# A two-layer model on one core: the picked experts' tiles fetched, scattered and summed another way, and r read from PSUM

## The reference

```python
# first layer, attention part (RWKV form), 16 heads of 16 channels
h  = rms_norm(x)                      # x is the layer norm of the input
xx = shift_by_one_token(h) - h
r, k, v = (h + xx*mu_r) @ Wr, (h + xx*mu_k) @ Wk, (h + xx*mu_v) @ Wv
decay = exp(-exp(w0 + tanh((h + xx*mu_w) @ wA) @ wB))
for t in tokens:                      # for each head a 16 x 16 state S
    kv = k[t][:, None] * v[t][None, :]
    o[t] = r[t] @ (S + u * kv)
    S = decay[t][:, None] * S + kv
x = x + (group_norm(o) * silu(g)) @ Wo
x = x + gelu(rms_norm(x) @ ffn_w1) @ ffn_w2
# first layer, expert part: 2 shared experts, and the 4 best of 16 for each token
gate = top4(softmax(xt @ router_w.T)) # xt is the layer norm of x
x = x + shared(xt) + sum_e gate[e] * (gelu(xt @ up[e].T) @ down[e].T)
# second layer: a selective scan (512 channels x 16 states), then 2 groups of 32 experts, 2 picked
```

## Time and profile before

| | us |
|---|---|
| median of 3 runs | 5431.09 |
| the profiled execution, own time | 5400.89 |
| its span | 5399.1 |
| PE, DVE, ACT, POOL busy | 4088.6, 3766.1, 2723.4, 3324.5 |
| mean granted clock of PE | 0.876 of full |

### The profile page before, as it was taken

The page is one execution under the profiler, slowest core; times in us unless marked ns, Lnnn a source line. Parts: engine busy times, 40 slices in busy tenths (PEclk is TensorE's granted clock), DMA queues, the critical chain, the costliest instruction groups (busy, mean ns, idle before and its releaser), DMA issues. The chain is left out here.

```text
span 5399.1 us, 63470 instructions
## 1 busy us (share of the span) xinstructions
PE 4088.6 (76%) x18842; PEld 2739.3 (51%) x18842; DVE 3766.1 (70%) x6401; ACT 2723.4 (50%) x5744; POOL 3324.5 (62%) x2226
## 2 busy tenths in 40 slices
PE   5777777877688767778251698889888889759994
PEld 1344445554455534555241465555555555548883
DVE  6888886769777777631000698888888889845677
ACT  1333334543344434446131677777777777525552
POOL 3455554446666566651425888888888888845552
PEclk7877788887798878889676899999999999879997
DMA  3222234333455444542555311221122111187788
GB/s 140 86 97 96 97 116 136 122 127 119 126 161 142 127 140 128 159 129 73 117 127 101 99 54 65 80 85 68 63 79 81 69 66 70 58 252 236 229 282 281
DMA packets 425042, 658.92 MB, mean 122 GB/s; under 512 B 46688, under 2 KB 292832, under 8 KB 414688
## 3 DMA queue, kind: packets, MB, share of 16 engines
q1 hardware_dynamic: 347904, 509.95, 29.5%
q0 software_dynamic: 76800, 144.90, 10.2%
HBM read 450.83 MB, written 213.04 MB: 123 GB/s over the span
## 5 line engine op out<-in xcount | busy, mean ns | idle before, releaser
L1699 POOL TENSOR_TENSOR c_dbx<-c_dtx,c_Brep 128x1024 f32<-128x1024 f32 x512 | 1201.6, 2362 | 182.1 <-DVE c_hs L1717 99.5
L1127 POOL TENSOR_TENSOR a_kv<-a_rk,a_kv 128x512 f32<-128x512 f32 x512 | 731.8, 1447 | 864.4 <-DMA a_kv<-v_rows 852.7
L1717 DVE TENSOR_TENSOR_SCAN c_hs<-psum,c_carry,c_dbx 128x512 f32<-128x512 f32 x768 | 937.4, 1266 | 119.4 <-ACT psum L1706 70.4
L1706 ACT ACTIVATE psum<-c_dt,c_cols 128x512 f32<-128x512 f32 x1024 | 697.2, 688 | 363.2 <-DVE c_hs L1717 358.7
L1136 DVE TENSOR_TENSOR_SCAN a_S<-a_decay,a_carry,a_kv 128x513 f32<-128x513 f32 x512 | 795.5, 1554 | 60.8 <-POOL a_kv L1127 55.5
L1733 PE MATMUL psum<-ident,c_hs 128*128 128x128 f32 x4096 | 609.0, 282 | 110.3 <-DVE c_hs L1717 106.6
L1733 PEld LDWEIGHTS psum<-ident,c_hs 128*128 128x128 f32 x4096 | 486.0, 144 | 393.3 <-DVE c_hs L1717 215.3
L1142 DVE TENSOR_TENSOR a_prod<-a_rk,a_S 128x512 f32<-128x512 f32 x512 | 454.8, 888 | 140.3 <-PE psum L1158 140.3
L1048 POOL DMA_INDIRECT a_xc<-picked_results,a_from_row x192 | 343.1, 1787 | 227.3 <-DMA a_xc<-x 130.4
L2128 POOL DMA_INDIRECT results<-d_ys,d_to_row x320 | 310.9, 972 | 236.1 <-DVE d_to_row L2228 178.6
L892 POOL DMA_INDIRECT picked_rows<-a_row,a_to_row x256 | 342.5, 1338 | 176.5 <-DVE a_xb L705 80.1
(11 more groups left out here) (321 smaller groups left out, 8593.9 us busy)
## 6 DMA issues: line engine op xcount, KB each, us to landing
a_kv<-v_rows SPq DMA_DIRECT2D x512, 256.0 KB
c_Brep<-b_rows SPq DMA_DIRECT2D x64, 1024.0 KB, 4.7
a_t_rows<-picked_rows SPq DMA_DIRECT2D x316, 136.0 KB, 2.3
d_xs<-sorted_rows SPq DMA_DIRECT2D x320, 128.5 KB
picked_results<-a_t_y SPq DMA_DIRECT2D x316, 128.0 KB
d_w<-results SPq DMA_DIRECT2D x64, 512.0 KB, 11.4
d_w<-in_d_experts SPq DMA_DIRECT2D x32, 768.0 KB, 9.4
x<-a_xb SPq DMA_DIRECT2D x20, 512.0 KB, 3.5
```

The lines of the kernel that those rows point to most:

```text
L1127: m_kv[g] = pool.mark(nc.gpsimd.tensor_tensor(kv[:, g % NV, 1:C + 1], rk[slot][:, 1, hb, :], kv[:, g % NV, 1:C + 1], ALU.mult))
L1699: m_dbx[g] = m_dbx[g + 1] = pool.mark(nc.gpsimd.tensor_tensor(dbx[:, r:r + 2, :], dtx[slot][:, e, :].unsqueeze(1).broadcast_to([P, 2, C]), ...
L1706: m_da[g] = act.mark(nc.scalar.activation(psum[:, DA + g % ND, :], dt[slot][:, e, :], ACT.Exp, scale=A[:, e, n:n + 1]))
L1717: m_scan[q] = dve.mark(nc.vector.tensor_tensor_scan(hs[:, q % NR, :], psum[:, DA + q % ND, :], dbx[:, q % NX, :], first, ALU.mult, ALU.add))
```

## The change

Two things are changed in the first layer.

1. Picked experts. The segments are 2, 3, 4, 4 and 3 chunks. A routed row now carries, beside its 16 gates, 16 slot numbers (token x 4 + rank of the pick), so that it is 288 values wide. ACT issues the fetch of each tile. The step's instructions have another order. POOL copies the slot column of a tile to `to_slot` and scatters the tile's results with an indirect DMA to their slots; there are 4 buffers `t_y` and not 2. `combine` is then 4 plain DMAs of POOL for a chunk, DRAM to DRAM, which add the results of pick k to x; each waits for the one before it. The correction of row numbers in `plan`, the gathers, `xc` and the quota are gone.
2. The scan. The ring `G` has 3 banks (5 to 7). Banks 3 and 4 hold r of the current chunk: ACT copies it there (`queries`), and the product behind the scan reads r from the bank. The copy into `carry` is done by ACT.

Besides, the load of `xa` is a generator of its own (`ask_xa`), `SORT_RATE` is 1.0 and not 0.8, and the list of streams is longer.

```diff
+        def ask_xa(c):
+            while now[0] < (c - 2) * steps + steps // 2 or c >= 3 and not is_done(("x1 free", c - 3)):
+                yield
+            load_xa(c)
+            m_done["xa asked", c] = True
...
-        OB, FD, G = 0, Banks(psum, 2, 1), Banks(psum, 3, 5)
+        OB, FD, RB, G = 0, Banks(psum, 2, 1), 3, Banks(psum, 5, 3)
...
+        def queries(c):
+            for hb in range(KB):
+                while not is_done(("r", c)) or c >= 1 and not is_done(("used r", c - 1, hb)):
+                    yield
+                yield from rest(1)
+                act.after(m_done["r", c], m_done.get(("used r", c - 1, hb)))
+                m_done["r bank", c, hb] = act.mark(nc.scalar.copy(psum[:, RB + hb, :], rk[c % 2][:, 0, hb, :]))
...
-                    sp.after(m_T.get(q - NTX), m_ty.get(q - NTX))
-                    nc.sync.dma_start(t_rows[:, q % NTX, :], row_of[bass.ds(at_row.pop(j), 1), :, :].rearrange("a p d -> p (a d)")).then_inc(s_tx[q % NTX], 16)
+                    act.after(m_T.get(q - NTX), m_ty.get(q - NTX), m_slot.get(q - NTX))
+                    nc.scalar.dma_start(t_rows[:, q % NTX, :], row_of[bass.ds(at_row.pop(j), 1), :, :].rearrange("a p d -> p (a d)")).then_inc(s_tx[q % NTX], 16)
...
-                    sp.after(m_ty[q])
-                    nc.sync.dma_start(result_of[j], t_y[:, q % NTY, :]).then_inc(s_ty[q % NTY], 16)
+                    pool.after_alone(m_ty[q], m_slot[q])
+                    nc.gpsimd.indirect_dma_start(out=picked_results[slot], in_=t_y[:, q % NTY, :], in_offset=None,
+                                                 out_offset=bass.IndirectOffsetOnAxis(ap=to_slot[:, q % NTI:q % NTI + 1], axis=0),
+                                                 bounds_check=Z.results - 1).then_inc(s_ty[q % NTY], 16)
...
+                        if q - 3 >= NTI:
+                            pool.engine.wait_ge(s_ty[(q - 3 - NTI) % NTY], 16 * ((q - 3 - NTI) // NTY + 1))
+                        pool.engine.wait_ge(s_tx[(q - 3) % NTX], 16 * ((q - 3) // NTX + 1))
+                        m_slot[q - 3] = pool.mark(nc.gpsimd.tensor_copy(to_slot[:, (q - 3) % NTI:(q - 3) % NTI + 1], t_rows[:, (q - 3) % NTX, E:][:, bass.ds(at_slot.pop(j), 1)]))
...
+            pool.engine.wait_ge(s_store[c % 2], 16 * (c // 2 + 1))
+            for i in range(NTY):
+                pool.engine.wait_ge(s_ty[i], 16 * len(range(i, m_done["tiles", s], NTY)))
+            at = (c - opens[s]) * C * TOP
+            results_of = picked_results[s % 2][at:at + C * TOP, :].rearrange("(p t k) d -> p t k d", t=TL, k=TOP)
             for k in range(TOP):
...
+                if k:
+                    yield from rest(3)
+                    pool.engine.wait_ge(s_sum[c % 4], 16 * (c // 4 * TOP + k))
+                nc.gpsimd.dma_start(chunk_of(chunks_out, c), results_of[:, :, k, :], accum_op=ALU.add).then_inc(s_sum[c % 4], 16)
+                yield
...
-                    dve.after(m_scan[q], m_sum.get((q - NP) // 4 * 4 + 3))
-                    m_prod[q] = dve.mark(nc.vector.tensor_tensor(prod[:, q % NP, :], rk[cq % 2][:, 0, sq_ // DK, :], S[:, q % NS, 0:C], ALU.mult))
+                    dve.after(m_scan[q], m_sum.get((q - NP) // 4 * 4 + 3), m_done["r bank", cq, sq_ // DK])
+                    m_prod[q] = dve.mark(nc.vector.tensor_tensor(prod[:, q % NP, :], psum[:, RB + sq_ // DK, :], S[:, q % NS, 0:C], ALU.mult))
...
-                    dve.after(m_scan[q])
-                    m_kept[q] = dve.mark(nc.vector.tensor_copy(carry[:, q % steps - 3:q % steps + 1], S[:, q % NS - 3:q % NS + 1, C]))
+                    act.after(m_scan[q])
+                    m_kept[q] = act.mark(nc.scalar.copy(carry[:, q % steps - 3:q % steps + 1], S[:, q % NS - 3:q % NS + 1, C]))
...
-    SEGMENTS = [4, 4, 4, 4]
+    SEGMENTS = [2, 3, 4, 4, 3]
```

More of the change, by code:

```diff
@@ L1 @@
-import math
 from contextlib import ExitStack
@@ L830, in plan @@
             i, bank = yield from G.claim(pe)
-            pe.after(m, m_moves)
-            m_moved = pe.mark(nc.tensor.matmul(bank[:, 2 * NT:2 * NT + E], ones[0:E, :], moves[:, :], start=True, stop=True))
+            pe.after(m, m_skip)
             pe.mark(nc.tensor.matmul(bank[0:1, 0:NT], ones[0:E, 0:1], past[:, :], start=True, stop=True))
@@ L939, in tiles @@
                 held = {}
-                for step in range(total + 5):
-                    if 0 <= step - 4 < total:
-                        store(step - 4)
+                for step in range(total + 6):
+                    if 0 <= step - 5 < total:
+                        store(step - 5)
                     if step + 2 < total:
@@ L945, in tiles @@
                     q = begun + step
+                    if 0 <= step - 3 < total:
+                        i, bank = held["hT"]
+                        act.after(m_hx[q - 3], m_dn.get(q - 3 - NTH))
+                        m_hT[q - 3] = G.freed[i] = act.mark(nc.scalar.copy(t_hT[:, (q - 3) % NTH, :], bank[:, 0:P]))
                     if step < total:
-                        tiles_begun[0] += 1
                         i, bank = yield from G.claim(pe)
@@ L1011, in combine @@
         def combine(c):
-            s, last_segment = segment_of[c], c >= opens[-1]
-            while not is_done(("tiles", s), ("out", c)) or c >= 1 and not is_done(("final", c - 2 if last_segment else c - 1)):
+            s = segment_of[c]
+            while not is_done(("tiles", s), ("out", c)) or c >= 4 and not is_done(("final", c - 4)):
                 yield
-            pool.after(m_done["rows", s])
-            if c in opens or last_segment:
-                for i in range(NTY):
-                    pool.engine.wait_ge(s_ty[i], 16 * len(range(i, m_done["tiles", s], NTY)))
@@ L1185, in prepare @@
             def prepare():
-                main, chain, inputs, ahead, sort = [], [], [], [first] if c == 0 else [], []
+                main, chain, inputs, ahead, sort, reads = [], [], [], [first] if c == 0 else [], [], [first_r] if c == 0 else []
+                asks = []
                 if c >= 1:
-                    main.append(block_work(c - 1, Z.quota(c)))
+                    main.append(block_work(c - 1))
                     chain.append(attention_out(c - 1))
@@ L1206, in layer0_phase @@
         left.streams[5][2].append(scatter(last))
-        for side in range(2):
-            left.streams.append([1.0, 0.0, [combine(c) for c in range(opens[-1], NCH) if c % 2 == side]])
+        for c in range(opens[-1], NCH):
+            left.streams.append([1.0, 0.0, [combine(c)]])
         while not is_done(("normed", last, 1)):
```

219 lines of the change are left out of this document (83 added, 136 removed).

## The result

The changed kernel took 5299.2 us (median of 4 runs) against 5436.0 before (median over the same chip's runs): ratio 0.9745, interval 0.9712 to 0.9778. It is 2.5% faster. The forecast of 5255 us named the sign and was 44 us too low; its range held the time. Its inner sum was less good: the tail gave more than foreseen, and the scan stage, forecast unchanged, became 120 us longer.

A forecast was written before the change was run, and what follows sets the result against it. VectorE bounds early scan chunks nearly alone, coupled in-order queues the later ones; VectorE idles in the tail. Scan stage 0, tail -173: 5400.9 to 5228, plus 30 for the median 5258, written 5255; range 5080 to 5470.

The forecast's parts named there:

- the tail: First layer from scan's end to second layer: +30 to the last plan, -130 last segment's tiles, -73 sums, total -173 us.
- the scan stage: First layer's 16 chunks of scan steps, 44 to 2346 us: -100 + 60 + 20 + 25 - 20 + 15 = 0.
- r out of PSUM: Scan stage: products at 0.68 us, 107 less, and carry copies off VectorE, 52.8; of 160 us relief, 100 taken.
- The carry: Scan stage: every fourth scan waits for the copy in ScalarE's queue; +60 us, ends 0 and 160.
- the test I set on it: Scan's total wait for ScalarE's carry copy: under 100 us means forecast right, over 230 means (a).
- Rival (a): Scan chained to ScalarE's queue by the carry copy: scan stage grows by 274 us, total 5532; chance 0.20.
- Three banks: Scan stage: three banks in place of five, tile step holding one at a time; +20 us, ends 0 and 100.
- Fetches on ScalarE: Scan stage: issue of 331 tile fetches makes ScalarE later; counted inside the carry's ends, of which 60 us taken.
- POOL, SP and the tiles: Scan stage: POOL's scatters and sums +25 us, SP's lighter queue -20, earlier tiles (214 done by scan's end) +15.
- the end of -70: Tail, last segment's tiles: gain only 70 us, not 130, if the previous segment's DRAM sums delay POOL's scatters.
- The sums: End of tail: 12 DRAM sums at 5 us plus 5 to land, 65 us in place of 138: -73.
- Rival (c): End of tail: DRAM sums slow, 120 us instead of 65, total 5313; chance 0.15.

The follow-up runs named there:

- the best kernel: The changed kernel with r read from SBUF, VectorE copying the carry, five banks, tile fetches on SyncE and segments of four chunks: 0.9333 to before, 5066.7 us.

## Why the prediction was right or wrong

In the order of the experiments the change is a chain of steps. The us are the differences of ratios times 5434; each carries about 14 to 24 us of uncertainty. Stage and tail are from the profiled runs, the first two steps across chips.

```
                                          ratio    step, us   stage   tail
picked experts alone, fetches on SyncE    0.9448   -300        -28    -266
  + fetches issued by ScalarE             0.9676   +124       +101     +34
  + three banks, not five                 0.9834    +86        +89       0
  + r read from PSUM                      0.9751    -45        -43      +6
  + carry copied by ScalarE (= changed)   0.9745     -3         +1      +2
```

- **r out of PSUM.** Mechanism right: 664 ns a product, against 680 foreseen. The Trainium skill, "SBUF — State Buffer", section "Who interferes with whom", says that a VectorE instruction with two SBUF inputs contends with GpSimd and one with at most one does not; the runs agree for the product (longest 693 ns against 2865) and for the scan, which keeps two and stays at a mean of 1527 (1554 before, longest now 4290). Size: 45 us, where I had 100 for it and the carry together. Before any tile exists the relief does show: by 480 us the changed kernel had done 117 products and the kernel before 110, from starts at 53.6 and 56.7, which is some 117 and 123 us a chunk (120 to 128 foreseen). The yield is lost later.
- **The carry.** I had +60 for the wait and a share of the relief for the 52.8 us taken off VectorE. Together they are nothing, in both kernels. Taken net, relief and carry were -40 in the forecast and -48 in the runs. Wrong was the test I set on it: a total of waits for one releaser does not price them. Rival (a), at 0.20, did not happen; its symptom did.
- **Three banks.** The mis-sized term: 20 foreseen (ends 0 and 100), 86 measured. I read the one largest wait of the tile product, 34.8 us, and reasoned that a tile holds one bank at a time. But tiles, feed-forward and attention share the three, and a claim waits until the bank's last user has read it; for the tiles' transposes that was ScalarE's read, 32.5 us that the five banks do not show.
- **Fetches on ScalarE.** The step that failed. I had counted their issue as a part of ScalarE's lateness at the carry, inside the 60, and not as a price of its own. They cost 124 us with five banks and 70 in the changed kernel; in the scan stage they are +101 in the chain, for which its forecast had no term. The Trainium skill, "DMA: Bandwidth & Descriptors", section "Issuing engines are not separate DMA queues", says that another issuing engine saves only its issue time; that held no loss, and I took none from it. (The DMA engines that I called about half busy are at 28 to 53% in the earlier trace rows.) What the runs show is the other side: 339 ns of issue with its waits and gaps, 0.64 us a turn where the loop is closed through ScalarE.
- **POOL, SP and the tiles.** Forecast +25 - 20 + 15. With these parts alone, and SyncE's fetches, the stage ends 28 us earlier than before (2316.0 against 2343.9), some 10 of which are the chip's; so they gain and do not cost. POOL's wait for the v rows fell from 852.7 to 419.1 us. And 242 tiles were done by the scan's end, 28 more than the 214 that I had expected.
- **The tail, by its three parts.** To the last plan: 199.9 us for 224.8, -25 where I had +30; 26 tiles and not 54 were left for it. The last segment: 191.0 to the last tile, for 293.6 (-103; forecast -130). The tiles ran at 2.5 us and not at 2.1, for two reasons: the sums of the segment before beside the first of them, which I had named as the end of -70, and ScalarE's fetches (rows below). With SyncE's fetches and five banks the same stretch took 173.8. The sums: 52.4 for 149.2, -97, forecast -73. Together -224, forecast -173. Rival (c), slow sums, did not happen.

The tile rate, in the columns of the earlier trace rows (there 51 tiles in 103 us): two stretches of the last segment in the changed kernel, and one in the best kernel.

```profile
2720.00:2780.00 60.00, 8.51 (x18) 0.64 0.87 168
2780.00:2855.00 75.00, 16.22 (x35) 0.99 0.39 117
```
```profile
2509.00:2600.50 91.50, 24.87 (x53) 1.00 0.52 156
```

The first stretch takes 3.3 us a tile, the second 2.1, the best kernel 1.73. The 16 DRAM sums of the segment before were issued from 2665.2 on, 8 of them in the first stretch and none in the second. In the first the DMA engines are 87% busy and the granted clock is 0.64. The kernel with SyncE's fetches and five banks is slow there too, 3.0 us a tile beside the sums (23 in 70 us, clock 0.78) and 1.7 after them. So the slow half of the segment is not the fetches' work. How much of it is the DMA engines and how much the clock, no run tells.

The account of the number: from the 5228 forecast for the profiled execution to the 5308.0 measured are 80 us, +120 in the scan stage, -51 in the tail and +11 in the second layer (5305.9 - 2907.3 = 2398.6, before 5399.1 - 3011.5 = 2387.6). The median was forecast 30 above its profiled execution and lies 9 below, and 5258 was written as 5255. That leaves the 44. The test that called the prediction wrong "if the scan stage changes by more than 80 us either way" was met: the scan stage changed by 120. The number came out near by luck, because the tail paid for the stage.

## What to carry to other kernels

A large total of waits behind one releaser says where an engine's slack is, not what the releaser costs: put the operation back and see whether the waits only change their name. Before a DMA is moved to an engine that computes, look for the closed loop through that engine (a copy, the product that reads it, the copy of its result): there the issue and every wait ahead of it can be paid once a turn, even where the engine is idle for half of the stage. And a bank taken from a shared pool is priced by who claims banks in that stretch, not by the largest single wait with all of them there.

## What the runs showed of the hardware

Sums in DRAM were cheap at the end: 12 DMAs of 512 KB, each added to what lies there, were issued from 2859.53 and had landed by 2896.53, 3.1 us each (5 had been assumed), in a stretch with the DMA engines 97% busy. The last issue and the first work after it:

```profile
2888.76 1.15 POOL L1024 DMA_DIRECT2D x<-picked_results  x1 [1.58 <-DMA x<-picked_results]
2896.53 0.36 SPq L195 DMA_DIRECT2D c_W_out<-in_c_W_out  x1
```

The small copy of the carry is steadier on ScalarE but not shorter: 197 ns in the median there, 164 on VectorE, whose mean of 412 comes from long cases of up to 2222 ns. Its shortest, median and longest ns, in the kernel before and in the changed one, and the copy of r into PSUM, which took 596 ns where I had 680:

```profile
L1148 DVE COPY a_carry<-a_S x128: 149/164/2222, 65.2 to 2343.8; 128x4 f32<-128x4 f32 x128
```
```profile
L1119 ACT COPY a_carry<-a_S x128: 178/197/212, 60.1 to 2469.0; 128x4 f32<-128x4 f32 x128
L568 ACT COPY psum<-a_rk 128x512 f32<-128x512 f32 x30 | 17.9, 596 | 11.9 <-DVE a_prod L1111 11.8
```
